# SP fetches 148 chunks of source rows one row at a time, beside GpSimd's gathers, in a five-pass graph network

## The reference

```python
# layer 0
aggr = segment_sum(x[src], dst, N);  h = elu((x + aggr) @ W1 + b1);  out = h @ W2 + b2
# layer 1
msg = relu(concat(x[src], x[dst], edge_features) @ mW1 + mb1) @ mW2 + mb2
out = relu(concat(x, segment_sum(msg, dst, N)) @ uW1 + ub1) @ uW2 + ub2
# layer 2: two mean aggregations with a batch norm and a relu between them
h = l2norm(mean(x[src]) @ Wl1 + b1 + x @ Wr1);  h = relu(batchnorm(h))
out = l2norm(l2norm(mean(h[src]) @ Wl2 + b2 + h @ Wr2) + x)
# layer 3: a 64x64 matrix per edge type (16 types)
out = segment_sum(x[src] @ weight[etype], dst, N)
```

## Time and profile before

| | us |
|---|---|
| Median of 3 runs | 9930.19 |
| Lowest and highest run | 9926.19, 9943.86 |
| The profiled execution's own time | 9929.83 |
| Its span | 9928.0 |
| GpSimd (POOL) busy | 7381.4 (74%) |
| TensorE matmul (PE) busy | 5057.8 (51%) |
| VectorE (DVE) busy | 2602.1 (26%) |
| ScalarE (ACT) busy | 1280.8 (13%) |

### The profile page before, as it was taken

One profiled execution on the slowest core, in us unless ns is written; L12 is line 12 of the kernel. 1 busy time (PEld: TensorE's weight loads), 2 busy tenths in 40 slices (PEclk: granted clock), 3 DMA queues, 4 the chain that ended last, 5 costly groups with the idle time before them and its releaser, 6 DMA issues.

```text
span 9928.0 us, 68540 instructions
## 1 busy us (share of the span) xinstructions
PE 5057.8 (51%) x23622; PEld 4285.6 (43%) x23623; DVE 2602.1 (26%) x5963; ACT 1280.8 (13%) x2646; POOL 7381.4 (74%) x7823
## 2 busy tenths in 40 slices
PE   4555555566666666344444445666666633323333
PEld 3444444456666666333333334444555422222222
DVE  2222222233444443111111113333333311111111
ACT  1111111111111111000000001222222200000000
POOL 7777777767777777677777777777777667777777
PEclk6555555577777777555555555555555555555555
DMA  3111111133333333111111112222222211111111
GB/s 73 33 33 34 33 33 34 32 88 92 93 93 93 93 93 87 27 30 30 30 30 30 30 29 68 78 78 81 79 79 80 76 29 28 28 28 29 28 28 28
DMA packets 396618, 525.10 MB, mean 53 GB/s; under 512 B 175674, under 2 KB 232868, under 8 KB 396200
## 3 DMA queue, kind: packets, MB, share of 16 engines
q0 software_dynamic: 250080, 359.01, 16.0%
q1 hardware_dynamic: 56929, 81.63, 2.8%
q10 hardware_dynamic: 89255, 80.01, 2.6%
HBM read 442.81 MB, written 77.29 MB: 52 GB/s over the span
## 4 chain that ended last, share of the span: by engine, by line
POOL 74%; issue 25%; PE 1%; DVE 0%; DMA 0%; ACT 0%; ACTq 0%; POOLq 0%; DVEq 0%
POOL G L436 74%; PE PAG L1095 0%; PE NB L1095 0%; PE NA L1095 0%; PE PH L1095 0%; DMA G<-in_x,SRC 0%; DMA near_tab<-STG 0%; DVE FA L715 0%; DMA G<-rel_tab,IDX 0%; DMA h_tab<-STG 0%; ACT L503 0%; DMA G<-far_tab,SRC 0%; DMA G<-h_tab,SRC 0%; DVE HT L1031 0%; DMA G<-x_tab,SRC 0%
## 5 line engine op out<-in xcount | busy, mean ns | idle before, releaser
L1095 PE MATMUL PAG<-OH,G 128*64 128x96 f32 (+2 forms) x12544 | 2369.8, 383 | 3844.0 <-DMA G<-rel_tab,IDX 1370.1
L1095 PEld LDWEIGHTS PAG<-OH,G 128*64 128x64 f32 (+2 forms) x12544 | 2167.4, 253 | 4094.6 <-issue 3623.9
L436 POOL DMA_INDIRECT G<-rel_tab,IDX x1563 | 1474.7, 944 | 525.5 <-issue 525.5
L436 POOL DMA_INDIRECT G<-far_tab,SRC x1563 | 1474.9, 944 | 515.6 <-issue 476.1
L436 POOL DMA_INDIRECT G<-x_tab,SRC x1563 | 1475.5, 944 | 503.3 <-issue 476.0
L436 POOL DMA_INDIRECT G<-h_tab,SRC x1563 | 1475.0, 944 | 498.0 <-issue 475.7
L436 POOL DMA_INDIRECT G<-in_x,SRC x1563 | 1479.0, 946 | 476.1 <-issue 475.2
L779 DVE TENSOR_TENSOR AGG<-AGG,PAG 64x96 f32 (+2 forms) x980 | 245.6, 251 | 5510.9 <-PE PAG L1095 5501.0
L1095 PE MATMUL PAG<-OH,HT 128*128 128x96 f32 x3136 | 652.6, 393 | 630.2 <-ACT HT L614 630.2
L748 DVE TENSOR_TENSOR OH<-CONST,DREL 128x768 f32<-128x768 f32 x981 | 927.9, 946 | 3.7 <-issue 2.7
L1095 PEld LDWEIGHTS PAG<-OH,HT 128*128 128x128 f32 x3136 | 607.3, 297 | 678.0 <-ACT HT L614 677.6
(11 more groups left out here) (151 smaller groups left out, 3840.1 us busy)
## 6 DMA issues: line engine op xcount, KB each, us to landing
rel_tab<-STG ACTq DMA_DIRECT2D x100, 500.0 KB
HT<-dst_rows SPq DMA_DIRECT2D x196, 192.0 KB
HT<-in_efT SPq DMA_DIRECT2D x196, 128.0 KB
G<-in_x,SRC POOLq DMA_INDIRECT x1563
G<-far_tab,SRC POOLq DMA_INDIRECT x1563
G<-x_tab,SRC POOLq DMA_INDIRECT x1563
G<-h_tab,SRC POOLq DMA_INDIRECT x1563
G<-rel_tab,IDX POOLq DMA_INDIRECT x1563
```

The lines of the kernel that those rows point to most:

```text
L436: pool.indirect_dma_start(out=G[:, h, j, 0:tabs[p].shape[1]], out_offset=None, in_=tabs[p], in_offset=bass.IndirectOffsetOnAxis(ap=numbers ...
L1095: return nc.tensor.matmul(dst, lhsT, rhs, start=start, stop=stop, skip_group_check=True)
```

## The change

SP takes over the last chunk of every sixth super (in pass 1 of every eighth; in pass 0 from super 30 on). For each of the chunk's 128 edges it issues one load of one row, whose byte address it has in a register, into one partition of a new buffer `GROWS` (three places). That is 28, 24, 32, 32 and 32 chunks in the five passes, 148 in all, and 18,944 loads. GpSimd issues seven gathers instead of eight for such a super.

In pass 0 SP begins once `prep` has reached its last value; in passes 2 to 4 it begins with the table's last write, as GpSimd does. In pass 1 it issues 16 row loads behind each `stream_straight`. Three new index tables hold byte addresses: `SRC_E` and `IDX3_E` for rows of 64 floats and `WIDE_E` for rows of 128. The vector engine makes them in five more steps of `prep`, and two more small arrays are loaded at the start. The users of these supers wait for `row_in` and read the eighth chunk from `GROWS`; the vector and scalar operations of passes 1 and 3 are split in a part of seven chunks and a part of one. GpSimd's gathers from super 24 of pass 0 on stand behind a branch on `REGULAR_I`.

```diff
-SPANS_READY, ROWS_READY, PREP_READY, TABLES_READY = 5, 43, 45, 48
+SPANS_READY, ROWS_READY, PREP_READY, TABLES_READY = 5, 43, 45, 53
+ROW_BUFS = 3
+SHARED = 24
+ROW_SUPERS = [range(SHARED + 6, SUPERS - 1, 6), range(8, SUPERS - 1, 8)] + [range(6, SUPERS - 1, 6)] * 3
...
+        SRC_E = sb("SRC_E", [SUPERS // 2, P], I32)
+        WIDE_E = sb("WIDE_E", [SUPERS // 2, P], I32)
+        IDX3_E = sb("IDX3_E", [SUPERS // 2, P], I32)
+        GROWS = sb("GROWS", [P, ROW_BUFS, P])
...
-            sp.wait_ge(rows_out, ROWS_OUT)
             sp.wait_ge(prep, TABLES_READY)
-            sp.wait_ge(stored[0], all_stored(0))
+            def row_starts(p, s, e):
+                registers = row_registers[e // SLOTS % 2]
+                starts = (SRC_E, WIDE_E, SRC_E, WIDE_E, IDX3_E)[p]
+                sp.reg_load(registers, starts[s // 2:s // 2 + 1, e:e + SLOTS])
+                last = 4 * tabs[p].shape[1] * (tabs[p].shape[0] - 1)
+                return [sp.snap(r, min_val=0, max_val=last) for r in registers]
+            def row(p, k, e, start):
+                b = k % ROW_BUFS
+                w = tabs[p].shape[1]
+                table = tabs[p].rearrange("n c -> (n c)").bitcast(U8)
+                sp.dma_start(GROWS[e:e + 1, b, 0:w].bitcast(U8), table[bass.ds(start, 4 * w)].unsqueeze(0))\
+                  .then_inc(row_in[p][b], 16)
+            def row_buffer_free(p, k):
+                if k >= ROW_BUFS:
+                    before = ROW_SUPERS[p][k - ROW_BUFS]
+                    if p == 1:
+                        sp.wait_ge(mixed, SLOTS + before + 1)
+                    else:
+                        sp.wait_ge(summed, SUPERS * p + SLOTS + before + 1)
+            def some_rows(p, lo, hi):
+                for at in range(lo, hi, SLOTS):
+                    k, e = at // P, at % P
+                    if e == 0:
+                        row_buffer_free(p, k)
+                    for i, start in enumerate(row_starts(p, ROW_SUPERS[p][k], e)):
+                        row(p, k, e + i, start)
...
             with sp.If(regular > 0):
+                some_rows(0, 0, P * len(ROW_SUPERS[0]))
+                sp.wait_ge(rows_out, ROWS_OUT)
+                sp.wait_ge(stored[0], all_stored(0))
+                piece = P // (ROW_SUPERS[1][1] - ROW_SUPERS[1][0])
                 for s in range(SUPERS):
...
                     stream_straight(s, starts[s % SLOTS])
+                    if (s + 1) * piece <= P * len(ROW_SUPERS[1]):
+                        some_rows(1, s * piece, (s + 1) * piece)
+                for p in range(2, LAYERS):
+                    sp.wait_ge(stored[p - 1], all_stored(p - 1))
+                    some_rows(p, 0, P * len(ROW_SUPERS[p]))
...
-            def gathers(p, s):
+            def gathers(p, s, by_rows=()):
-                filled = max(1, min(GROUP, FILLED - s * GROUP))
+                filled = GROUP - 1 if s in by_rows else max(1, min(GROUP, FILLED - s * GROUP))
...
+            pool.wait_ge(prep, TABLES_READY)
+            regular = is_regular(pool)
+            with pool.If(regular > 0):
+                layers(ROW_SUPERS)
...
+            link(nc.vector.tensor_scalar(DI[0:SUPERS // 2, 0:P], SRC_E[:, :], float(R), None, ALU.mult))
+            link(nc.vector.tensor_tensor(IDX3_E[:, :], IDX3_E[:, :], DI[0:SUPERS // 2, 0:P], ALU.add))
+            link(nc.vector.tensor_scalar(WIDE_E[:, :], SRC_E[:, :], 4.0 * H, None, ALU.mult))
+            link(nc.vector.tensor_scalar(SRC_E[:, :], SRC_E[:, :], 4.0 * D, None, ALU.mult))
+            link(nc.vector.tensor_scalar(IDX3_E[:, :], IDX3_E[:, :], 4.0 * D, None, ALU.mult))
...
+                b = None
+                if p != 1 and s in ROW_SUPERS[p]:
+                    b, landed = row_buffer(p, s)
+                    if p != 3:
+                        pe.wait_ge(row_in[p][b], landed)
+                sum_window(p, h, m, b).then_inc(summed, 1)
```

More of the change, by code:

```diff
@@ L231, in gnn_kernel @@
         gathered = [sem(f"gathered{h}") for h in range(SLOTS)]
+        row_in = [[sem(f"row_in{p}_{b}") for b in range(ROW_BUFS)] for p in range(LAYERS)]
         onehot_ready = sem("onehot_ready")
@@ L439, in gathers, with layers @@
                     ).then_inc(gathered[h], 16 * (GROUP - j if j == filled - 1 else 1))
-            pool.wait_ge(first_in, 16)
[L442 to L454, removed]
-                        pool.wait_ge(prep, SPANS_READY)
-                        nc.gpsimd.partition_all_reduce(MR, MM, P, RMAX).then_inc(spans_out, 1)
-                    if p == 0 and s == SLOTS - 1:
-                        pool.wait_ge(src_in, 16)
+            def layers(rows):
+                for p in range(LAYERS):
+                    if p == 1:
+                        pool.wait_ge(stored[0], all_stored(0))
+                    if p == 2:
+                        pool.wait_ge(stored[1], all_stored(1))
+                    if p == 3:
+                        pool.wait_ge(stored[2], all_stored(2))
+                    if p == 4:
+                        pool.wait_ge(stored[3], all_stored(3))
+                    for s in range(0 if p else SHARED, SUPERS):
+                        gathers(p, s, rows[p])
+            pool.wait_ge(first_in, 16)
+            for s in range(SHARED):
+                gathers(0, s)
+                if s == 0:
+                    pool.wait_ge(prep, SPANS_READY)
+                    nc.gpsimd.partition_all_reduce(MR, MM, P, RMAX).then_inc(spans_out, 1)
+                if s == SLOTS - 1:
+                    pool.wait_ge(src_in, 16)
+            pool.wait_ge(prep, TABLES_READY)
+            regular = is_regular(pool)
+            with pool.If(regular > 0):
+                layers(ROW_SUPERS)
+            with pool.If(regular < 1):
+                layers([()] * LAYERS)
         @block.scalar
@@ L616, in straight @@
                             act.wait_ge(bn_shifted, s + 1)
[L617 removed]
+                            chunks = GROUP
+                            if s in ROW_SUPERS[3]:
+                                chunks = GROUP - 1
+                                b, landed = row_buffer(3, s)
+                                nc.scalar.activation(GROWS[:, b, :], GROWS[:, b, :], ACT.Relu)
+                            nc.scalar.activation(G[:, h, 0:chunks, :], G[:, h, 0:chunks, :], ACT.Relu)\
+                              .then_inc(bn_relu, 1)
                         for u, stage in SCHEDULE[s]:
@@ L1117, in _, with sum_window @@
                 pe.reg_mov(reg, 0)
-            def sum_window(p, h, m):
+            def sum_window(p, h, m, by_rows=None):
                 msg = HID[:, h % 2, :].rearrange("p (j c) -> p j c", j=GROUP) if p == 1 else G[:, h, :, :]
                 for j in range(GROUP):
-                    last = mm(PAG[0:m, 0:WIN], msg[:, j, 0:m], OH[:, h % 2, j, :], j == 0, j == GROUP - 1)
+                    rows_ = msg[:, j, 0:m]
+                    if j == GROUP - 1 and by_rows is not None:
+                        rows_ = GROWS[:, by_rows, 0:m]
+                    last = mm(PAG[0:m, 0:WIN], rows_, OH[:, h % 2, j, :], j == 0, j == GROUP - 1)
                 return last
```

49 lines of the change are left out of this document (38 added, 11 removed).

## The result

The kernel with the change takes 10,711.13 us (median of 4 runs, 10,652.56 to 10,734.11), the one before 9928.60 (4 runs, 9926.19 to 9943.86): a ratio of 1.0779, 95% interval 1.0750 to 1.0808. It is 783 us slower; 9749 was forecast, and the range ended at 9960. The profiled execution is the fastest of the four; what makes the others up to 82 us longer stands in no trace.

A forecast was written before the change was run, and what follows sets the result against it. GpSimd's back-to-back gathers were taken to bound the kernel, before and, by 3 ns a row, after the change. 9929.8 - 184.8 for removed gathers + 4 for additions = 9749 us; range 9738 to 9960.

The forecast's parts named there:

- The 148 gathers by 1.2485 us: GpSimd, all passes: 148 gathers fewer at 1.2485 us from start to start, 184.8 us saved if SP's rows arrive in time.
- The law of the passes: Each pass: SP's row time must stay under a limit: 0.495 or 0.498 us in pass 0, 0.52 in 1, 0.463 in 2 to 4.
- T: SP's time per one-row load with its share of the register load: 0.464 us by its terms, taken as 0.46.
- The threshold of 0.463: Passes 2 to 4: SP keeps GpSimd's pace up to 0.463 us a row; each nanosecond more costs 4.1 us a pass.
- The break-even of 0.478: Passes 2 to 4: at 0.478 us a row, 15 ns past the limit, all of the 184.8 us gain is gone.
- SP is the bound, and the kernel is slower: Row loads of passes 2 to 4, from 0.478 us a row: 9958, about 10,520 or 10,834 us; chance 0.19.
- the first term of T: SP, before every four rows: register load 0.298, `snap` 0.096 and two gaps of 0.04, together 0.119 us a row.
- MOVE and gaps: SP, ahead of each row's load: a MOVE of 0.029 us and two gaps of 0.04, 0.109 us a row.
- row load: SP's load of one row: 0.23 us, the lowest of four seen at the start; bounds 0.19 and 0.29.
- code supply and the rest of the mean: SP waiting for code: 0.3 to 0.4 us once in 51 rows, 0.006 us a row.
- The bounds of T (0.42, 0.52, 0.60): SP's time per row: 0.42 us with a load of 0.19, 0.52 with 0.29, 0.60 if the product stays too.
- the product: SP, before each row load: a FUSED_REGOPS multiplying row number by row length, left out; 0.077 us more if it stays.

The follow-up runs named there:

- e_load16_c: The changed kernel with sixteen registers in one register load instead of four, run beside a kernel before of 9927.67 us: 9802.70 us, ratio 0.9877.
- e_load8: The changed kernel with eight registers in one register load instead of four, all else as it is: 9917.65 us, ratio 0.9992.
- m4_loads: The kernel before, with short series of register loads and row loads added on SP at the start of pass 2, where it is idle: 9929.73 us.
- e_static: The changed kernel without register loads, `snap` and MOVE; every row load has a fixed address, all 18,944 stay: 9745.71 us, ratio 0.9817.

## Why the prediction was wrong

**What held.** The 148 gathers by 1.2485 us, on the path where SP keeps pace: 9745.7 with fixed addresses, 9790.7 with 117 chunks, 9754.1 with 140. The law of the passes: pass 1 had T up to 0.52 and came out at -29.9. Pass 0 had 0.498; there T is some 0.526 (3200 rows from super 30's use at about 330 us to 2012), which by 28 ns x 3200 costs 90 us, and -35.0 became +49.9 with the gap behind it, 85 us. Pass 2: 54 ns past 0.463 at 4.1 us are 221, minus the 40 saved 181; measured 155.4 + 15.2 in the gap behind it. The threshold of 0.463 can be checked in pass 3, the one pass that has several values of T past it: 0.475, 0.495 and 0.559 (e_load16_c, e_load8, the kernel after) made it 42, 118 and 372 us longer than GpSimd's own 1910.4. That is 3.8 to 4.0 us a nanosecond, 4.1 forecast, and it comes to nothing at some 0.465. The break-even of 0.478, which takes the same T for all passes, was met by no run. And the rival "SP is the bound, and the kernel is slower" gave 10,520 for T = 0.52; it was the right case, with a chance of 0.19, but for another cause than it named. With the measured T the prediction's own law gives 9749 + 54 x 12.3 + 90 = 10,503, and 10,680 with the 177 us of pass 3 below; the profiled execution took 10,652.56. (The rival's 3136 rows in pass 1 should be 24 x 128 = 3072; that is 1 us.)

**The step that failed** is the first term of T, "Four rows share one register load and one `snap`: 0.298 and 0.096 us". T's terms, in us a row:

| term | forecast | measured |
|---|---|---|
| register load, `snap`, gaps | 0.119 | (0.564 + 0.091 + 0.08) / 4 = 0.184 |
| MOVE and gaps | 0.109 | 0.092 |
| row load | 0.23 | 0.231 (0.265 behind the load, 3 x 0.220) |
| code supply and the rest of the mean | 0.006 | 0.010 |
| T | 0.464, taken as 0.46 | 0.517 |

The measured 0.092 is what the median of 2.027 us from one register load to the next leaves, in passes 0 and 2 to 4. All terms but one are within 0.017 and nearly cancel. With 0.298 in the first one T would be 0.517 - 0.0665 = 0.450, and the kernel would have kept pace in all passes but pass 3: e_load8, with T = 0.455, does just that. The duration had been read from 49 rows that agreed within 0.025 us, but all 49 stood behind the same neighbour, loads of other shapes; no row load was ever between two of them. The bounds of T (0.42, 0.52, 0.60) varied the row load and the product and held this term fixed. With 3 ns a row in hand it could be 12 ns longer; it was 266.

The Trainium skill had it. "DMA: Bandwidth & Descriptors", section "Latency and other measured facts", gives some 600 ns as the floor of a register load; the prediction reckoned T = 0.54 by it and set it aside on the strength of the earlier trace rows. The trace after agrees with the Trainium skill within a tenth: 0.564 us behind a row load. By these runs it is not a floor, though: 0.298 stands in the earlier trace rows, 0.302 in m4_loads. Both figures are true, each in its place.

**The second miss,** not in any case of the prediction: in pass 3 SP's own instructions are stretched behind the writes of `rel_tab`. With T at 0.517 that is the difference between pass 3 and pass 2, 332.4 - 155.4 = 177.0 us; with T at 0.455 it is 118 of the 139 by which e_load8's profiled span (9882.6) exceeds e_static's (9743.6); with 0.435 it is 42. Without it the change would still be slower, by 722.7 - 177.0 = 546 us. But the forecast gain would have been lost to it alone, too: e_load8 has the T that was forecast and no gain, 9917.65 us against 9927.36. The prediction's sum has no term for it and takes one T for all passes.

So the 722.7 us are: pass 0 and its gap 49.9, pass 1 and its gap -27.3, pass 2 and its gap 170.6, pass 3 and its gap 364.0, pass 4 and the end 165.5.

## What to carry to other kernels

A duration taken from a trace belongs to its place: before it is multiplied by thousands, look at what stood before it there and what will stand before it here, and bound it like any other unknown, with the figure of the Trainium skill as one end where it differs. Where a step has a pace to keep, work out first how many nanoseconds are left, and put the registers into as few loads as fit: 16 instead of four took a row from 0.517 to 0.43 us. And leave room for the pass in which another engine writes large tables.

## What the runs showed of the hardware

- A register load on SP behind a row load takes 0.50 us for one register, 0.564 for four, 0.797 for eight and 1.256 for 16, from four on 0.06 for each further one. Four registers take 0.29 to 0.32 where no row load has stood since the last register load and they come from partitions 0 to 60; from 64 to 100 it is 0.46 to 0.50 there. Behind a row load the partition makes no difference.
- SP issues a load of one row in 0.220 us with 0.1 us between two, and in 0.252 with 0.04 between: 0.31 and 0.29 from start to start. 18,944 of them beside the gathers changed no gather's 0.944 us.
- SP's instructions are stretched while 500 KB writes of ScalarE's queue move their packets: register loads up to 3.27 us, 175 us in all for 100 writes (580 us of packets) and 349 for 200 (1180), and 163 to 175 whether SP issues 256, 512 or 1024 register loads beside them.
- A row of 64 floats that SP loads from HBM makes two packets, of 256 and 4 bytes, which take 0.016 and 0.009 us.
- On two chips runs were met in which SP stands still for 0.7 or 1.4 us again and again: the same kernel takes 11,531 to 11,534 us there instead of 9928. One of them ran it in 9927.67 at another time, so it is no fixed property of the chip.
